# A two-layer transformer block on one core: the end in another order, and twelve gated products moved from VectorE to GpSimd

## The chip, the cores and the metric

The kernel runs on one core of one Trainium2 chip. The metric is the device time of one execution in microseconds (us), as a median over the runs. Times inside the kernel come from one profiled execution; its clock starts with its first instruction.

## The reference

The input is x of shape (8, 256, 128): 8 sequences of 256 tokens, 128 features, float32. Four sub-layers follow one another, each with a residual and a layer norm without weights. Cut to what matters:

```python
x = _layernorm(x + _L0_attn_ref(x, ...))   # 16 heads of 8, full softmax
x = _layernorm(x + _L0_ffn_ref(x, ...))    # expand to 512, butterflies, gelu
x = _layernorm(x + _L1_attn_ref(x, ...))   # low-rank q, k, v, rope, causal softmax
x = _layernorm(x + _L1_ffn_ref(x, ...))

def _L1_ffn_ref(x, w_gate, w_up, w_down):  # integer weights times 1/127
    gate = jnp.einsum('bsd,hd->bsh', x, wg)    # 128 -> 384
    up = jnp.einsum('bsd,hd->bsh', x, wu)
    h = jax.nn.silu(gate) * up
    return jnp.einsum('bsh,dh->bsd', h, wd)    # 384 -> 128
```

The change concerns the last of these, the gated feed-forward layer of layer 1, and the order of the last steps.

## The kernel before, in words

The program is written out by hand for five engines: TensorE, ScalarE (`act`), VectorE (`dve`), GpSimd (`pool`) and SyncE (`sp`, transfers). Each engine has its own instruction order; semaphores hold them together. A semaphore is counted up by an instruction with `then_inc`, and `wait_ge` holds an engine until a count is reached. Everything that stands behind a wait in that engine's order waits too.

The work is cut into 16 batches: batches 0 to 7 are the 8 sequences in layer 0, batches 8 to 15 the same sequences in layer 1. A batch has 16 heads, so there are 256 heads. All engines run the same loop `for g in STEPS` (`g` = 0, 4, 8, ... 288), one step for four heads (QUAD). In a step with `g` below 256 TensorE computes the scores of heads g to g+3, and, 12 heads ahead (LEAD), those from which VectorE takes the maxima (L864 in layer 0, L872 in layer 1, where a masked copy is needed); ScalarE takes the exponentials (L760). In layer 1 GpSimd sets what the causal mask hides to zero (L1083), one step later. Every other piece of work hangs on the step `g` = 16 b + offset of batch b, on all engines: value products (L632) with VectorE's transposes (L954), normalisation of the attention on GpSimd (L1090) with a transpose on VectorE (L969), projection out (L608), residual and statistics (L946, L833), layer norm on GpSimd (`normalise`, L1017 to L1024), turning of the tokens on TensorE (L561) with the copy on ScalarE (L773). The order of the `if` blocks inside a step is the order within that step on each engine. The rotation of queries and keys (L1137 to L1139), the subtraction of their high parts (L1063) and VectorE's small high/low subtraction of the maxima (L887) prepare later batches; there are no batches after 15, so they stop with g = 212 on GpSimd.

The feed-forward layer of layer 1 is set by the table FFN1 (L52 to L54): for each batch three offsets for its three chunks of 128 hidden features, one for the down matmuls, and one for the layer norm. For batch b and chunk c, with i = 3 (b - 8) + c:

- TensorE (L578 to L588) claims a bank and does four matmuls in 128x256 pieces, gate features into columns 0 to 255 and up features into 256 to 511. The bank's next user waits for `hid_ready`.
- ScalarE (L785 to L791) takes tanh of half the gate into `th` (two buffers).
- VectorE (`gate`, L889 to L901) makes `gated` = (th + 1) * gate, waits for itself (`link`), and multiplies it by the up features in the bank into `hid1`. The factor 0.5 of silu lies in the down weights. `th`, `gated` and `hid1` have two buffers each (`hid1` by batch).
- TensorE (L589 to L599) does the down matmuls from `hid1`; VectorE adds the residual (L935) and takes statistics; GpSimd normalises at the third number of the table; SyncE stores the batch.

Four gates of batches 13 and 14 are issued by VectorE at steps of their own (`LATE_GATES`, L56, L995), at the end of steps 260, 264 and 268. Up to step 252 a bank for such work is given by place; from step 256 on all banks are claimed in turn, eight of them. At the end of the kernel: step 264 on TensorE has the ups of (14,1), the down matmuls of batch 13 and the projection out of batch 15, in this order; step 268 the turn of batch 15 and the ups of (14,2); step 272 the ups of batch 15; steps 276 and 280 the down matmuls of batches 14 and 15. The layer norm of the attention of batch 15 and the last two of the feed-forward layer are divided: GpSimd takes the power -0.5, VectorE the subtraction and multiplication (`normalise_last`, L843).

In the profile `gated` appears as `room_c` (it shares that room with other tiles), `hid1` as `hid`, and all PSUM banks as `bank`.

Of the kernel before, what the change touches and what calls it, by code (L numbers as in the profile page):

```python
# [52 lines left out]
FFN1.update({BATCHES - 4: ((40, 40, 52), 60, 64), BATCHES - 3: ((40, 44, 52), 56, 64),  # L53
             BATCHES - 2: ((36, 40, 44), 52, 56), BATCHES - 1: ((32, 32, 32), 40, 44)})  # L54
# [70 lines left out]
def ffn1_at(g, i):  # L125

    for b in FFN1:
        if g == H * b + FFN1[b][i]:
            return b
    return None  # L130

# [19 lines left out]
def block_kernel(nc, x_nat, x_t, wfirst, bfirst, wqk0, wv0, bqk0, bv0, wproj, bproj, u0, d0, fac_u, fac_d, bfw, bup, bcon, bdown,  # L151
# [7 lines left out]
    with ctx:  # L159
# [3 lines left out]
        def sem(name):  # L163
            return ctx.enter_context(nc.semaphore(name))
# [19 lines left out]
        def part(room, first, shape):  # L184
# [83 lines left out]
            "up_ps", "th_ready", "hid_ready", "down_ps", "res_done", "var_ready", "ln_ready")}  # L268
# [3 lines left out]
        stored = [sem(f"stored{i}") for i in range(2)]  # L272

# [8 lines left out]
        def layer(b):  # L282
            return b // NB
# [69 lines left out]
        def _(pe):  # L353
# [172 lines left out]


# [18 lines left out]
            for g in STEPS:  # L546
# [10 lines left out]
                if (b := turned_at(g)) is not None:  # L557
                    bank = claim(("xt", b), A["xt_ready"], b + 1, g)
                    pe.wait_ge(A["ln_ready"], b + 1)
                    for q in range(QT):  # L560
                        ins = nc.tensor.transpose(bank[:, q * P:(q + 1) * P], NA["ln"][:, b % LN_RING, q, :], id32[:, :])  # L561
                    ins.then_inc(A["xt_ps"], 1)
# [15 lines left out]
                for b, c in ups_at(g):  # L578
                    i = b - NB
                    bank = claim(("up1", i, c), F1["hid_ready"], SC * i + c + 1, g)  # L580
                    if c == 0:
                        pe.wait_ge(A["xt_ready"], b + 1)
                        if i == 0:
                            pe.wait_ge(wf_ready, 2)
                    for s in range(2):
                        ins = nc.tensor.matmul(bank[:, s * T:(s + 1) * T], wf[:, s, c * P:(c + 1) * P],  # L586
                                               xt[:, i * T:(i + 1) * T], start=True, stop=True)
                    ins.then_inc(F1["up_ps"], 1)  # L588
                if (b := ffn1_at(g, 1)) is not None:  # L589
                    i = b - NB  # L590
                    bank = claim(("dn1", i), F1["res_done"], i + 1, g)
                    pe.wait_ge(F1["hid_ready"], SC * (i + 1) - (1 if b == BATCHES - 1 else 0))
                    for q in range(QT):
                        for c in range(SC):
                            if q == 0 and c == SC - 1 and b == BATCHES - 1:
                                pe.wait_ge(F1["hid_ready"], SC * (i + 1))
                            ins = nc.tensor.matmul(bank[:, q * W:(q + 1) * W], hid1[:, i % 2, c, q * P:(q + 1) * P],  # L597
                                                   wf[:, 2, c * W:(c + 1) * W], start=(c == 0), stop=(c == SC - 1))
                    ins.then_inc(F1["down_ps"], 1)  # L599
                if (b := attention_at(g, AT_PROJ)) is not None:  # L600
                    bank = claim(("proj", b), A["res_done"], b + 1, g)
                    pe.wait_ge(A["att_ready"], b + 1)
                    if b == 0:
                        pe.wait_ge(ld["bv"], 32)
                    elif b == NB:
                        pe.wait_ge(ld["next"], 64)
                    for q in range(QT):
                        ins = nc.tensor.matmul(bank[:, q * P:(q + 1) * P], att[:, q * P:(q + 1) * P],  # L608
                                               (wproj_sb if layer(b) == 0 else wout_sb)[:, :], start=True, stop=True)
                    ins.then_inc(A["proj_ps"], 1)  # L610
# [73 lines left out]
        def _(act):  # L684
# [68 lines left out]
            for g in STEPS:  # L753
# [31 lines left out]
                for b, c in ups_at(g):  # L785
                    i = SC * (b - NB) + c
                    act.wait_ge(F1["up_ps"], i + 1)
                    if i >= 2:
                        act.wait_ge(F1["hid_ready"], i - 1)
                    act.activation(th[:, i % 2, :], g_bank["up1", b - NB, c][:, 0:T], ACT.Tanh, scale=0.5)\  # L790
                        .then_inc(F1["th_ready"], 1)  # L791
# [30 lines left out]
        def _(dve):  # L822
# [66 lines left out]
            def gate(b, c):  # L889
# [3 lines left out]
                dve.wait_ge(F1["th_ready"], i + 1)  # L893
                if c == 0 and b >= NB + 2:
                    dve.wait_ge(F1["down_ps"], b - NB - 1)
                if i >= 2:
                    dve.wait_ge(F1["hid_ready"], i - 1)
                link(nc.vector.scalar_tensor_tensor(out=gated[:, i % 2, :], in0=th[:, i % 2, :], scalar=1.0,  # L898
                                                    in1=bank[:, 0:T], op0=ALU.add, op1=ALU.mult))
# [107 lines left out]
        def _(pool):  # L1007
# [62 lines left out]
            for g in STEPS:  # L1070
# [26 lines left out]
                if (b := ffn1_at(g, 2)) is not None and b >= HURRY:  # L1097
                    pool.wait_ge(F1["var_ready"], b - NB + 1)
                    inverse(N1 if b < BATCHES - 1 else NL, QT).then_inc(last_ready, 1)
                if (b := attention_at(g, AT_LN)) is not None and b < BATCHES - 1:  # L1100
# [193 lines left out]
```

## Time and profile before

| what | value |
|---|---|
| median of 3 runs | 326.21 us (324.72 to 326.78) |
| the profiled execution's own time | 325.87 us |
| its span, first to last instruction | 324.1 us |
| mean granted TensorE clock | 0.959 |
| TensorE busy | 275.0 us (85%) |
| VectorE busy | 253.7 us (78%) |
| ScalarE busy | 216.5 us (67%) |
| GpSimd busy | 205.3 us (63%) |

Busy is the time in which an engine has an instruction under way; shares are of the span and are means over stages that differ. The granted clock is 1.00 at 2.4 GHz and 0.50 at 1.2 GHz. "A <- B" in a list of waits means that engine and line A stood still until B was done. Matmuls are pipelined, so their ends are modelled.

### The profile page before, as it was taken

The page shows a single profiled execution, that of the slowest core. Times are in us where ns is not written, and L with a number is a line of the kernel's source. Part 1 is how long each engine was busy: PE and PEld are TensorE (multiplying, and loading weights), DVE is VectorE, ACT ScalarE, POOL GpSimd, SP SyncE. Part 2 cuts the span into 40 slices and gives each one's busy share as a digit, 9 for nine tenths or more (in the row PEclk, how much of TensorE's full clock was granted, in tenths as well). Part 3 has the DMA queues.
Part 4 walks back from the last instruction along what each step waited for, and adds up shares of the span by engine and source line. Part 5 has one row for each costly group of instructions (what it writes and reads, how often), then busy time and mean ns, then how long its engine had stood idle before and what let it go on. Part 6 is the DMA issues. An engine that isn't in the chain of part 4 may idle for free.

```text
span 324.1 us, 9463 instructions
## 1 busy us (share of the span) xinstructions
PE 275.0 (85%) x3194; PEld 200.0 (62%) x3194; DVE 253.7 (78%) x991; ACT 216.5 (67%) x444; POOL 205.3 (63%) x326
## 2 busy tenths in 40 slices
PE   8989969988978999888998896988898787878763
PEld 4766646655565556554676565866676666667553
DVE  4778796886878778897676697598999999775555
ACT  2546883788976799499983999468685757444110
POOL 0529995472448546584779897498879747366332
PEclk9979997999999999999995999899999999899978
DMA  7784350303021130404013140401314040000000
GB/s 228 258 254 144 93 192 15 131 1 131 3 97 35 32 133 17 150 4 155 8 46 120 23 145 11 153 1 41 126 35 148 3 148 20 2 2 18 17 16 32
DMA packets 20495, 25.84 MB, mean 80 GB/s; under 512 B 3744, under 2 KB 14304, under 8 KB 20320
## 3 DMA queue, kind: packets, MB, share of 16 engines
q1 hardware_dynamic: 20016, 24.72, 22.9%
q8 instruction: 26, 0.43, 0.6%
q10 hardware_dynamic: 432, 0.53, 0.4%
q14 instruction: 21, 0.17, 0.2%
HBM read 6.36 MB, written 1.05 MB: 23 GB/s over the span
## 4 chain that ended last, share of the span: by engine, by line
PE 51%; DVE 25%; issue 12%; ACT 9%; POOL 2%; POOLq 0%; ACTq 0%; DVEq 0%
PE bank L632 14%; DVE mx L864 6%; PE bank L388 5%; PE bank L647 4%; DVE room_c L872 4%; ACT E L760 4%; PE bank L398 4%; PE bank L576 4%; PE bank L515 2%; PE bank L597 2%; DVE room_c L898 2%; PE bank L407 2%; PE bank L586 2%; DVE turned L954 2%; PE bank L608 2%
## 5 line engine op out<-in xcount | busy, mean ns | idle before, releaser
L760 ACT ACTIVATE E<-bank 128x512 f32<-128x512 f32 (+1 forms) x256 | 119.7, 549 | 65.4 <-PE bank L411 37.9
L864 DVE TENSOR_REDUCE mx<-bank 128x2 f32<-128x512 f32 x128 | 79.6, 681 | 13.0 <-PE bank L388 12.8
L872 DVE CUSTOM_DVE_ANT_0 room_c<-bank,mask_sb 128x256 f32<-128x256 f32 (+1 forms) x256 | 72.9, 349 | 2.3 <-PE bank L388 2.1
L388 PE MATMUL bank<-QK 32*128 32x256 f32 x480 | 56.0, 308 | 8.4 <-DVE mx L872 3.4
L398 PE MATMUL bank<-QK 32*128 32x256 f32 x480 | 51.8, 311 | 11.5 <-DVE hid L900 6.7
L632 PE MATMUL bank<-E,V 128*32 128x256 f32 (+1 forms) x1024 | 59.5, 376 | 0.2
L388 PEld LDWEIGHTS bank<-QK 32*128 32x128 f32 x480 | 38.4, 187 | 21.4 <-issue 8.9
L1083 POOL TENSOR_SCALAR_AFFINE_SELECT E<-E 128x512 f32<-128x512 f32 x64 | 39.2, 638 | 11.6 <-ACT E L760 11.6
L398 PEld LDWEIGHTS bank<-QK 32*128 32x128 f32 x480 | 35.1, 188 | 17.5 <-DVE hid L900 9.0
L632 PEld LDWEIGHTS bank<-E,V 128*32 128x32 f32 x1024 | 31.0, 115 | 20.7 <-issue 3.6
L954 DVE STREAM_TRANSPOSE turned<-bank 128x256 f32<-128x256 f32 x32 | 14.3, 447 | 21.2 <-PE bank L632 20.9
L407 PE MATMUL bank<-mt,const_r 32*128 32x512 f32 x128 | 26.9, 435 | 4.0 <-ACT mt L704 4.0
L1063 POOL TENSOR_TENSOR parts<-qk,parts 128x512 f32<-128x512 f32 x15 | 19.2, 1278 | 14.9 <-ACT parts L730 14.9
L586 PE MATMUL bank<-xt,wf 128*128 128x256 f32 x96 | 25.6, 410 | 2.1 <-ACT E L760 1.6
L1090 POOL TENSOR_TENSOR at<-turned,rec 128x256 f32<-128x256 f32 x16 | 10.1, 632 | 26.2 <-DVE rec L976 26.2
L411 PE MATMUL bank<-mt,const_r 32*128 32x256 f32 (+1 forms) x256 | 22.9, 281 | 0.0
L586 PEld LDWEIGHTS bank<-xt,wf 128*128 128x128 f32 x96 | 18.4, 202 | 5.8 <-ACT E L760 2.8
L872 DVE DVE_READ_ACCUMULATOR2_ANT mx<- 128x1 f32 x256 | 21.2, 83 | 0.0
L1021 POOL TENSOR_SCALAR nm_a<-mv_a 128x2 f32<-128x2 f32 x15 | 2.9, 194 | 28.3 <-DVE mv_a L836 28.3
L411 PEld LDWEIGHTS bank<-mt,const_r 32*128 32x128 f32 x256 | 18.7, 195 | 0.2 <-ACT mt L704 0.2
L767 ACT ACTIVATE QK<-spread_qk 128x1024 fp32r<-128x1024 f32 x16 | 17.2, 1078 | 0.0
L647 PE MATMUL bank<-down,room_a 128*128 128x128 f32 x128 | 17.0, 288 | 0.0
(127 smaller groups left out, 561.7 us busy)
## 6 DMA issues: line engine op xcount, KB each, us to landing
spread_qk<-parts SPq DMA_DIRECT2D x30, 256.0 KB, 2.5
spread_qk<-parts SPq DMA_DIRECT2D x60, 128.0 KB, 2.2
room_c<-room_c SPq DMA_DIRECT2D x64, 32.0 KB, 1.9
xb<-x_nat SPq DMA_DIRECT2D x1, 1024.0 KB, 7.1
out<-ln_g SPq DMA_DIRECT2D x7, 128.0 KB, 1.9
xt<-x_t SPq DMA_DIRECT2D x1, 768.0 KB, 7.1
wi<-wi_all SPq DMA_DIRECT2D x1, 576.0 KB, 3.5
room_c<-fac_u SPq DMA_DIRECT2D x1, 508.0 KB, 6.4
```

The lines of the kernel that those rows point to most:

```text
L388: ins = nc.tensor.matmul(g_bank["max", m][:, cols], both[:, 0, c * P:(c + 1) * P], both[:, 1, keys], start=True, stop=True)
L398: nc.tensor.matmul(g_bank["exp", m][:, c * T:(c + 1) * T - q0], both[:, 1, c * P:(c + 1) * P], both[:, 0, q0:T], start=(c == 0), stop=False)
L407: ins = nc.tensor.matmul(g_bank["exp", m][:, :].rearrange("p (c t) -> p c t", c=2), ones, most.unsqueeze(1).broadcast_to([STRIP, 2, T]), s ...
L411: ins = nc.tensor.matmul(g_bank["exp", m][:, c * T:(c + 1) * T - c * P], ones, most[:, c * P:T], start=False, stop=(c == 1))
L586: ins = nc.tensor.matmul(bank[:, s * T:(s + 1) * T], wf[:, s, c * P:(c + 1) * P], xt[:, i * T:(i + 1) * T], start=True, stop=True)
L632: ins = nc.tensor.matmul(bank[VCOL * j:VCOL * (j + 1), q0:T], values, E[:, (2 * n + e) % E_RING, j, k * T:(k + 1) * T - q0], start=(e == 0 ...
L647: ins = nc.tensor.matmul(bank[:, i * W:(i + 1) * W], hid0[:, c, s * P:(s + 1) * P], down[:, c, :], start=(c == 0), stop=(c == HC - 1))
L760: act.activation(E[:, a % E_RING, j, 0:n], g_bank["exp", m][:, 0:n], ACT.Exp, scale=SCALE)\
L864: ins = nc.vector.tensor_reduce(mx[:, n % 2, :, i], bank[:, :].rearrange("p (q k) -> p q k", q=QT), AX.X, ALU.max, negate=True)
L872: ins = nc.vector.tensor_tensor_reduce(out=masked_s[:, at % 2, lo:hi], in0=bank[:, lo:hi], in1=mask_sb[:, T + lo - hi:T], scale=-1.0, scal ...
L954: nc.vector.transpose(turned[:, t, :], g_bank["pv", n][:, 0:T]).then_inc(A["turned"], 1)
L1083: nc.gpsimd.affine_select(out=e, in_=e, pattern=[[0, 4], [1, P]], compare_op=ALU.is_ge, fill=0.0, base=0, channel_multiplier=-1).then_inc( ...
```

## The change

Three things are changed. The table FFN1 puts the down matmuls of batch 13 at step 268 instead of 264, and the ups of (14,2) at step 264 instead of 268. In TensorE's order of a step the projection out of batch 15 now comes ahead of turns, ups and downs, and the turn of batch 15 behind the down matmuls. So step 264 has the projection of batch 15, ups (14,1), ups (14,2); step 268 the down matmuls of batch 13 and then the turn of batch 15. VectorE's residual and statistics of batch 13 move to step 268 with them, behind the last normalisation of the attention.

For batches 8 to 11 (SHARED; 12 chunks) ScalarE first copies the up features from the bank into `hid1` and then takes the tanh; VectorE does only the first of the gate's two instructions and frees the bank; GpSimd multiplies `hid1` in place by `gated`, one step later, ahead of its layer norm of the attention and of the rotation. Batches 12 to 15 keep both instructions on VectorE.

```diff
-             BATCHES - 4: ((40, 40, 52), 60, 64), BATCHES - 3: ((40, 44, 52), 56, 64),
-             BATCHES - 2: ((36, 40, 44), 52, 56), BATCHES - 1: ((32, 32, 32), 40, 44)})
+             BATCHES - 4: ((40, 40, 52), 60, 64), BATCHES - 3: ((40, 44, 52), 60, 64),
+             BATCHES - 2: ((36, 40, 40), 52, 56), BATCHES - 1: ((32, 32, 32), 40, 44)})
+
+SHARED = range(NB, BATCHES - 4)
...
+def shared(i):
+
+    return i // SC + NB in SHARED
...
+        def hidden_done(i):
+
+            return (F1["product"], i + 1) if shared(i) else (F1["hid_ready"], i + 1 - SC * len(SHARED))
+
+        def gate_done(i):
+
+            return (F1["gated"], i + 1) if shared(i) else hidden_done(i)
...
-                if (b := turned_at(g)) is not None:
...
+                if (b := turned_at(g)) is not None and b < BATCHES - 1:
+                    turn_tokens(b, g)
+
+                if attention_at(g, AT_PROJ) == BATCHES - 1:
+                    project_out(BATCHES - 1, g)
...
-                    bank = claim(("up1", i, c), F1["hid_ready"], SC * i + c + 1, g)
+                    bank = claim(("up1", i, c), *gate_done(SC * i + c), g)
...
-                    pe.wait_ge(F1["hid_ready"], SC * (i + 1) - (1 if b == BATCHES - 1 else 0))
+                    pe.wait_ge(*hidden_done(SC * i + SC - (2 if b == BATCHES - 1 else 1)))
...
-                if (b := attention_at(g, AT_PROJ)) is not None:
...
+                if turned_at(g) == BATCHES - 1:
+                    turn_tokens(BATCHES - 1, g)
+                if (b := attention_at(g, AT_PROJ)) is not None and b < BATCHES - 1:
+                    project_out(b, g)
...
                     act.wait_ge(F1["up_ps"], i + 1)
+                    if shared(i):
+                        if c == 0 and b >= NB + 2:
+                            act.wait_ge(F1["down_ps"], b - NB - 1)
+                        act.activation(hid1[:, b % 2, c, :], g_bank["up1", b - NB, c][:, T:2 * T], ACT.Copy)
                     if i >= 2:
-                        act.wait_ge(F1["hid_ready"], i - 1)
+                        act.wait_ge(*gate_done(i - 2))
...
                 dve.wait_ge(F1["th_ready"], i + 1)
+                if i >= 2:
+                    dve.wait_ge(*hidden_done(i - 2))
+                ins = nc.vector.scalar_tensor_tensor(out=gated[:, i % 2, :], in0=th[:, i % 2, :], scalar=1.0,
+                                                     in1=bank[:, 0:T], op0=ALU.add, op1=ALU.mult)
+                if shared(i):
+                    ins.then_inc(F1["gated"], 1)
+                    return
+                link(ins)
...
+                for b, c in ups_at(g - QUAD):
+                    i = SC * (b - NB) + c
+                    if shared(i):
+                        pool.wait_ge(F1["gated"], i + 1)
+                        nc.gpsimd.tensor_tensor(hid1[:, b % 2, c, :], hid1[:, b % 2, c, :], gated[:, i % 2, :], ALU.mult)\
+                            .then_inc(F1["product"], 1)
```

## Rows read from the trace of the kernel before

**Rows 1.** Windows, two periods of layer 1; columns as the header says.
```profile
core 0: us, PE busy (x) PEld busy (x) DVE busy (x) ACT busy (x) POOL busy (x), PEclk, DMA share, GB/s
...
246.00:262.60 16.60, 13.69 (x198) 11.08 (x198) 15.96 (x89) 11.51 (x26) 13.10 (x23) 1.00 0.19 68
262.60:279.30 16.70, 13.73 (x198) 11.17 (x199) 16.07 (x89) 10.98 (x25) 9.34 (x19) 1.00 0.11 35
```
**Rows 2.** Waits, 207.6 to 259.7 us: us in total, times, longest us.
```profile
POOL at L1090 <- DVE rec L976: 5.1, 2, 4.3
PE bank L398 <- DVE hid L900: 4.6, 4, 1.4
POOL nm_g L1021 <- DVE mv_g L836: 2.9, 2, 1.5
...
POOL nm_a L1021 <- DVE mv_a L836: 1.3, 2, 0.9
```
**Rows 3.** Timeline of VectorE: start us, us, line, operation, out<-in, count.
```profile
260.85 0.41 DVE L898 SCALAR_TENSOR_TENSOR room_c<-th,bank 128x256 f32<-128x256 f32 x1
261.29 0.42 DVE L900 TENSOR_TENSOR hid<-bank,room_c 128x256 f32<-128x256 f32 x1
261.63 0.41 DVE L898 SCALAR_TENSOR_TENSOR room_c<-th,bank 128x256 f32<-128x256 f32 x1
...
262.42 0.43 DVE L969 STREAM_TRANSPOSE att<-at 128x256 f32<-128x256 f32 x1
```
**Rows 4.** Timeline of ScalarE, the same pair of gates.
```profile
259.76 0.38 ACT L790 ACTIVATE th<-bank 128x256 f32<-128x256 f32 x1
260.63 0.38 ACT L790 ACTIVATE th<-bank 128x256 f32<-128x256 f32 x1 [0.48 <-PE bank L586]
```
**Rows 5.** Source lines L1090, L1114, L1063 of GpSimd: duration ns min/median/max, starts, forms.
```profile
L1090 POOL TENSOR_TENSOR at<-turned,rec x16: 629/632/637, 39.6 to 302.9; 128x256 f32<-128x256 f32 x16
...
L1114 POOL TENSOR_TENSOR xb<-ln_a,bcon_sb x8: 724/736/747, 57.7 to 181.9; 128x256 f32<-128x256 f32 x8
...
L1063 POOL TENSOR_TENSOR parts<-qk,parts x15: 1267/1278/1301, 9.9 to 257.2; 128x512 f32<-128x512 f32 x15
```
**Rows 6.** Timelines of GpSimd and TensorE around two hand-overs.
```profile
219.11 0.88 POOL L1024 TENSOR_SCALAR ln_a<-r_a,nm_a,rstd_a 128x128 f32<-128x128 f32 x2
...
221.49 0.44 PE L561 MATMUL bank<-const_sb,ln_a 128*128 128x128 f32 x2
...
259.67 0.64 POOL L1090 TENSOR_TENSOR at<-turned,rec 128x256 f32<-128x256 f32 x1
```
**Rows 7.** Source line L887 of VectorE, the small high/low subtraction.
```profile
L887 DVE TENSOR_TENSOR mxp<-mx,mxp x32: 175/382/1205, 16.2 to 287.1; 128x16 fp32r<-128x16 f32 x32
```
**Rows 8.** Timeline of TensorE at the end.
```profile
304.92 1.58 PE L597 MATMUL bank<-wf,hid 128*128 128x128 f32 x12 [0.93 <-DVE hid L900]
306.33 0.61 PE L608 MATMUL bank<-wout_sb,att 128*128 128x128 f32 x4
310.58 0.41 PE L561 MATMUL bank<-const_sb,ln_a 128*128 128x128 f32 x2 [3.64 <-DVE ln_a L843]
310.82 5.30 PE L586 MATMUL bank<-xt,wf 128*128 128x256 f32 x16
```
**Rows 9.** Timeline of VectorE at the end.
```profile
303.56 0.45 DVE L969 STREAM_TRANSPOSE att<-at 128x256 f32<-128x256 f32 x1 [1.63 <-POOL at L1090]
...
306.98 0.42 DVE L946 TENSOR_TENSOR r_a<-bank,xb 128x256 f32<-128x256 f32 x1
307.32 0.48 DVE L833 BATCH_NORM_STATS2 stats_g<-r_g 128x6 f32<-128x128 f32 x2
...
309.83 0.60 DVE L843 TENSOR_SCALAR ln_a<-r_a,mv_a,rstd_a 128x128 f32<-128x128 f32 x2 [0.33 <-POOL rstd_a L1018]
...
318.85 0.42 DVE L935 TENSOR_TENSOR r_l<-bank,ln_a 128x256 f32<-128x256 f32 x1
```
**Rows 10.** Windows, two stretches at a granted clock of 0.50.
```profile
280.70:284.10 3.40, 3.40 (x45) 2.05 (x48) 1.88 (x11) 0.51 (x2) 1.22 (x2) 0.50 0.02 5
...
311.40:314.80 3.40, 3.40 (x10) 2.69 (x9) 1.28 (x4) 0.78 (x3) 0.60 (x2) 0.50 0.12 39
```

More of the change, by code:

```diff
@@ L52 @@
 FFN1 = {b: ((40, 40, 48), 64, 68) for b in range(NB, BATCHES)}
[L53 to L54 removed]
+FFN1.update({BATCHES - 4: ((40, 40, 52), 60, 64), BATCHES - 3: ((40, 44, 52), 60, 64),
+             BATCHES - 2: ((36, 40, 40), 52, 56), BATCHES - 1: ((32, 32, 32), 40, 44)})
+SHARED = range(NB, BATCHES - 4)
 LATE_GATES = {(BATCHES - 3, 2): HEADS + 4, (BATCHES - 2, 0): HEADS + 8, (BATCHES - 2, 1): HEADS + 12, (BATCHES - 2, 2): HEADS + 12}
@@ L267, in block_kernel @@
         F1 = {n: sem(f"f1_{n}") for n in (
-            "up_ps", "th_ready", "hid_ready", "down_ps", "res_done", "var_ready", "ln_ready")}
+            "up_ps", "th_ready", "gated", "product", "hid_ready", "down_ps", "res_done", "var_ready", "ln_ready")}
         spread_in = sem("spread_in")
@@ L525, in project_values, with turn_tokens, project_out @@
                 ins.then_inc(A["v_ps"], 1)
+            def turn_tokens(b, g):
+                bank = claim(("xt", b), A["xt_ready"], b + 1, g)
+                pe.wait_ge(A["ln_ready"], b + 1)
+                for q in range(QT):
+                    ins = nc.tensor.transpose(bank[:, q * P:(q + 1) * P], NA["ln"][:, b % LN_RING, q, :], id32[:, :])
+                ins.then_inc(A["xt_ps"], 1)
+            def project_out(b, g):
+                bank = claim(("proj", b), A["res_done"], b + 1, g)
+                pe.wait_ge(A["att_ready"], b + 1)
+                if b == 0:
+                    pe.wait_ge(ld["bv"], 32)
+                elif b == NB:
+                    pe.wait_ge(ld["next"], 64)
+                for q in range(QT):
+                    ins = nc.tensor.matmul(bank[:, q * P:(q + 1) * P], att[:, q * P:(q + 1) * P],
+                                           (wproj_sb if layer(b) == 0 else wout_sb)[:, :], start=True, stop=True)
+                ins.then_inc(A["proj_ps"], 1)
             pe.wait_ge(idle_ready, 1)
@@ L556, in _ @@
                     project(b, claim(("qk", b), semaphore, value, g))
-                if (b := turned_at(g)) is not None:
[L558 to L562, printed above, removed]
+                if (b := turned_at(g)) is not None and b < BATCHES - 1:
+                    turn_tokens(b, g)
+                if attention_at(g, AT_PROJ) == BATCHES - 1:
+                    project_out(BATCHES - 1, g)
                 if (n := tile_at(g, AT_XT0)) is not None:
@@ L595, in _ @@
                             if q == 0 and c == SC - 1 and b == BATCHES - 1:
-                                pe.wait_ge(F1["hid_ready"], SC * (i + 1))
+                                pe.wait_ge(*hidden_done(SC * i + SC - 1))
                             ins = nc.tensor.matmul(bank[:, q * W:(q + 1) * W], hid1[:, i % 2, c, q * P:(q + 1) * P],
@@ L599, in _ @@
                     ins.then_inc(F1["down_ps"], 1)
-                if (b := attention_at(g, AT_PROJ)) is not None:
[L601 to L610, printed above, removed]
+                if turned_at(g) == BATCHES - 1:
+                    turn_tokens(BATCHES - 1, g)
+                if (b := attention_at(g, AT_PROJ)) is not None and b < BATCHES - 1:
+                    project_out(b, g)
                 if (b := values_at(g)) is not None:
@@ L893, in gate @@
                 dve.wait_ge(F1["th_ready"], i + 1)
+                if i >= 2:
[6 more added lines that the diff above has]
+                link(ins)
                 if c == 0 and b >= NB + 2:
                     dve.wait_ge(F1["down_ps"], b - NB - 1)
[L896 to L899, printed above, removed]
                 nc.vector.tensor_tensor(hid1[:, b % 2, c, :], bank[:, T:2 * T], gated[:, i % 2, :], ALU.mult)\
```

## The prediction

> **What bounds the kernel now.** I read the windows by stage first, then who waited for whom, then the timelines of the engines, and for the end the chain that ended last. The profiled execution has a span of 324.1 us and a time of 325.87 us, 0.34 us under the median of the three runs (326.21 us), so I work in the span and add the difference to the median.
>
> Both edits touch only what comes after about 207 us. From there to 280 us, one batch of layer 1 takes one period of 16.6 to 16.7 us, and in a period VectorE is busy 96% of the time, TensorE 13.7 us, ScalarE 11.0 to 11.5 us [rows 1]. The waits say the same: TensorE waits for the product of the gate before a bank comes free, 4.6 us in four waits between 207.6 and 259.7 us [rows 2]. GpSimd is the engine to watch: 13.1 us busy in the period from 246 us, but 9.3 us in the next, which has no rotation of queries and keys any more [rows 1]. From 207.54 us, where it stopped waiting (the longer of the two waits for rec), until 259.67 us its whole idle time is 5.1 - 4.3 + 2.9 + 1.3 = 5.0 us [rows 2]. At the end, from 301 us, no engine is full: one batch goes through proj, norm, turn, up, gate, down in a line, and what stands in front of it in an engine's order counts.
>
> **Shared products: VectorE.** A gate of before is a scalar_tensor_tensor and, after a wait for its own engine, a tensor_tensor. In the pair of gates (11,0), (11,1) the instructions start at 260.85 and 261.29, the second gate at 261.63, and the next one at 262.42 [rows 3]: the first of a gate takes 0.44, the second 0.34 us, and the second gate 0.79 in all. The change leaves one instruction, whose pitch without the chained wait is 0.34 us: 0.44 us less per gate, 12 gates, 5.3 us.
>
> **ScalarE.** The copy of the up half has the shape of a tanh row, 128x256 from PSUM, 0.38 us [rows 4]; bounds 0.26 (if it overlaps its neighbour by a third) and 0.41. The first copy of a pair has cover: its tanh starts at 259.76 and VectorE gets to it at 260.85. The second has less: the matmuls let it start at 260.63, so its tanh ends at 261.0 now and 261.3 to 261.4 after, against 261.19 when VectorE would want it. I charge 0.1 us a pair, with 0.2 at most. What is left of the pair is 0.77 us, and 0.43 us of the third gate, 1.2 us a batch, 4.8 us for four. TensorE's wait in front of the next scores, 1.0 to 1.4 us, is longer than that, so it does not become the bound there. The bank is released after the gate instruction instead of after the product, which is the same instant by which VectorE is earlier.
>
> **GpSimd.** Twelve products of 128x256 with both operands in SBUF. The nearest rows are the attention's multiplication, 0.632 us, and the addition of a bias, 0.736; the 512-column subtraction takes 1.278, which is the upper end for one product [rows 5]. I take 0.64 us, with a pitch of 0.59 since consecutive GpSimd rows overlap by about 0.05. The lower end is VectorE's own 0.42 us [rows 3]. Nine products fall in front of the attention normalisation of batch 12 (259.67 us [rows 6]): 9 x 0.59 = 5.3 us, against 5.0 us of idle time. So GpSimd has no idle time left there, and this normalisation ends not at 260.31 but at 260.31 + 0.3 = 260.6 us. Behind it stand VectorE's transpose of the result (262.42 now) and everything after: it can come at 260.6, 1.8 us earlier, not 0.77 x 4 + 0.43 x 3 = 4.4 us earlier. So two fifths of that gain arrive. On the way there is one more collision: in batch 9, ln_a ends at 219.99 (start 219.11, 0.88 us) and TensorE turns it at 221.49 [rows 6]. With two products ahead of it ln_a ends near 221.2, while TensorE, 1.1 us earlier, wants it at 220.4; 0.8 us of gain are given back there, but they are not on the path if GpSimd is the bound. Behind batch 12's normalisation GpSimd is free again (9.3 us busy [rows 1]), and the third gate of batch 11 adds its 0.43. Shared part: 1.8 + 0.4 = 2.2 us.
>
> The multiplication on GpSimd takes 0.632 us where VectorE took 0.42 [rows 3, 5]: half as much again. The Trainium skill (GPSIMD Engine Reference, Engine selection) gives elementwise products to VectorE and calls GpSimd about 2x slower with two inputs; by that ratio a product would be an estimated 0.85 us and the shared part 9 x 0.21 = 1.9 us poorer, near nothing. I hold to the row. The Trainium skill (GPSIMD Engine Reference, Key points) has the two engines contend for SBUF where VectorE has two SBUF inputs. The small high/low subtraction is such an instruction, and its rows vary from 175 to 1205 ns with a median of 382 [rows 7], which fits. The gates read PSUM and are steady at 0.41 and 0.42 us.
>
> The waits that are added: ScalarE's copy of a first chunk waits for the down matmuls of two batches before, over 10 us past. A product waits for its gate, which is one GpSimd step old; behind it in GpSimd's order stand the layer norm of the attention, the rotation of queries and keys (which ScalarE's next copy of the projection and SyncE's transfers wait for), and the masks, without which the value matmuls can't start. A TensorE bank waits for the gate alone, the down matmuls for the product, 12 heads or more after it is issued.
>
> **The end in another order.** Before, TensorE does up (14,1) and down 13 (304.92, 1.58 us, held until the gate of (13,2)) before the projection of batch 15, at 306.33 [rows 8]. Its input, VectorE's transpose, is done at 303.56 + 0.45 = 304.01 [rows 9]. After, it goes first: 304.15 to 304.75, and the residual of batch 15 starts at 304.8 instead of 306.98, now without down 13's residual (0.42 us) and statistics in front. From residual to ln_a it is 2.85 us now, of which down 13's statistics (307.32, 0.48 us and their aggregation [rows 9]) take some 0.6, so 2.25 after: ln_a would start at 307.05 instead of 309.83, 2.8 us earlier. TensorE meanwhile has up (14,1) and (14,2), 8 matmuls or 2.0 us, and down 13, 1.5 us: 304.75 + 3.5 = 308.25. So the new order makes down 13 the last to hold back the turn, at 308.3 instead of 310.58: 2.3 us earlier. Then up (14,2), four of the 16 matmuls at 310.82, is out of the way: 12 remain, 3.1 us at the full clock, from 309.2 (copy of the turned tokens) to 312.3. Of the 5.30 us of the 16, 3.4 us ran at a granted clock of 0.50, the 1.2 GHz level (311.40 to 314.80 [rows 10]), behind a TensorE wait of 3.64 us that the new order fills. GpSimd's layer norm of batch 13 keeps its step, ends some 2 us after VectorE's statistics at 309.5, and only the residual of down 14 needs it, at 313.7. VectorE then has down 13's residual and statistics (308.3 to 309.5) and five gates of 0.8 us: 313.5, as late as TensorE's ups allow. Down 14 and 15 go 312.3 to 315.1, so the last residual starts at 315.2 instead of 318.85 [rows 9]: 3.7 us earlier at the full clock; with half clock for 3.4 us somewhere in it, 2.7. I take 3.4.
>
> **Sum.** 2.2 + 3.4 = 5.6 us: 325.87 - 5.6 = 320.3 in the profiled execution, 326.2 - 5.6 = 320.6 us as median.
>
> **Rivals.**
> (A) The sharing gives nothing, the end does. For it: GpSimd's 5.0 us of idle time lie in five pieces, each behind a wait of its own, and a product of 0.736 us instead (pitch 0.69) costs 0.9 us more; add the 0.8 us of ln_a. Against: the pieces are in order with the products. 326.2 - 3.4 = 322.8 us.
> (B) GpSimd is not the bound (products at VectorE's 0.42: 9 x 0.42 = 3.8 us, under 5.0). Then VectorE's gain of 4.8 us arrives less the 0.4 of collisions: 326.2 - 4.4 - 3.4 = 318.4 us.
> (C) The end gives half: turn and ups wait for down 13, or another stretch of half clock as the one at 280.70, in which TensorE was busy all 3.4 us [rows 10]. 326.2 - 2.2 - 1.7 = 322.3 us.
> (D) GpSimd becomes the bound and costs more than the rest brings. Place: attention normalisation of batches 10 to 12. At 1.24 us pitch the nine products take 11.2 us, 5.9 more than above, and a TensorE that waits so long falls to half clock as behind 3.64 us here [rows 8, 10], at most half of 3.4 us. 320.6 + 5.9 + 1.7 = 328.2 us. It decides from 1.2 us a product. Against: two rows of this size at 0.63 and 0.74.
>
> **How the numbers follow.** Forecast 0.47, A 0.19, B 0.13, C 0.16, D 0.05. A measurement of this kernel tells about 1% (3.3 us): faster below 322.9. The forecast, B, two thirds of C and half of A are faster (0.47 + 0.13 + 0.10 + 0.09 = 0.79); slower half of D, 0.03; the rest, 0.18, is the same. The range reaches from B's 318.4 less 0.6 to A with 0.8 us more: 317.8 to 323.6.
>
> **What would show it.** The scalar_tensor_tensor x24 with tensor_tensor only x12; twelve GpSimd products of 0.60 to 0.75 us; GpSimd without idle time from 207.5 to the multiplication of batch 12, near 260; the period of TensorE's wait at the pair of gates under 16.3 us and that wait near 0.5 us; a turn of batch 9 that waits for ln_a; in the last 25 us proj of batch 15 before down 13, no TensorE wait of 3 us behind it, and last residual to end of span unchanged at 5.3 us. It is wrong if the periods stay at 16.7 us (A), if products take over 0.8 us (D), or if the turn of batch 15 comes less than 1.5 us earlier against the attention's last transpose (C).

## The result and the profile after

The changed kernel takes 318.59 us (median of 6 runs, 317.29 to 319.34); the kernel before, run beside it, takes 325.47 us. The ratio is 0.977, 95% interval 0.974 to 0.980: 2.3% faster. The forecast was 320.6 us, with a range of 317.8 to 323.6. Some executions of any of these kernels run some per cent longer at a lower clock: the ratios leave them out, the medians hold them.

The page of the changed kernel, its span and its busy times:

```profile
span 317.1 us, 9471 instructions
...
PE 273.0 (86%) x3194; PEld 198.9 (63%) x3194; DVE 249.8 (79%) x979; ACT 219.5 (69%) x456; POOL 213.7 (67%) x338
...
PE 44%; DVE 19%; POOL 14%; issue 11%; ACT 9%; POOLq 0%; ACTq 0%; DVEq 0%
```

The last line is the chain that ended last, by engine. GpSimd has 14% of the span in it; before it had 2%. VectorE has 12 instructions fewer, ScalarE and GpSimd have 12 more.

Where the 7.0 us of span went is read best from five instructions that both kernels have: the attention's multiplication on GpSimd for batch 9, and VectorE's transposes (att) behind that multiplication for batches 12, 13, 14 and 15. Their start times, taken from the timelines, cut the span into six parts (us):

| kernel | start to mult. 9 | to att 12 | granted clock there | to att 13 | to att 14 | to att 15 | to the end |
|---|---|---|---|---|---|---|---|
| before | 207.54 | 54.88 | 1.00 | 16.65 | 13.31 | 11.18 | 20.54 |
| after | 207.20 | 54.55 | 0.97 | 16.19 | 11.81 | 11.17 | 16.18 |
| difference | -0.34 | -0.33 | | -0.46 | -1.50 | -0.01 | -4.36 |

The first part is the same work in both and its 0.34 us are no part of the change. The 1.50 us in front of att 14 are the half-clock stretch of [rows 10] at 280.70, which this execution has elsewhere. So the profiled pair shows 0.8 us for the sharing, 4.4 us for the end (the half-clock stretch behind the turn of batch 15 is in it, since it too is gone), and 1.5 us of clock elsewhere.

The windows of the changed kernel, the whole shared stretch, a half-clock stretch in it, two periods, and the end:

```profile
core 0: us, PE busy (x) PEld busy (x) DVE busy (x) ACT busy (x) POOL busy (x), PEclk, DMA share, GB/s
222.30:225.70 3.40, 3.25 (x53) 2.26 (x42) 1.62 (x9) 0.86 (x3) 3.40 (x5) 0.50 0.22 48
245.30:261.90 16.60, 13.51 (x198) 10.99 (x196) 15.36 (x85) 12.59 (x31) 16.00 (x27) 1.00 0.19 67
261.90:278.40 16.50, 13.95 (x204) 11.41 (x207) 15.94 (x89) 11.27 (x27) 12.41 (x24) 1.00 0.19 65
...
300.90:311.80 10.90, 9.66 (x62) 8.62 (x62) 9.73 (x32) 2.31 (x7) 2.86 (x7) 1.00 0.07 25
```

Against [rows 1], GpSimd is busy for 16.0 of the 16.6 us in the period from 245 us, where it was 13.1, and VectorE went from 16.0 to 15.4. Who waited for whom between 207.3 and 261.1 us (us in total, times, longest):

```profile
POOL at L1125 <- DVE rec L1011: 4.3, 1, 4.3
...
PE bank L413 <- DVE room_c L927: 2.3, 4, 0.8
PE bank L547 <- POOL ln_a L1059: 1.9, 2, 1.0
...
POOL hid L1139 <- DVE room_c L927: 0.7, 1, 0.7
```

The waits behind mv_g and mv_a of [rows 2] are gone: GpSimd is late for them now. The wait for rec is the one of 4.3 us in front of the stretch, so GpSimd's time in waits fell from 5.0 to 0.7 us. TensorE waits for the bank 2.3 us instead of 4.6, and a new wait stands there, 1.9 us for ln_a before the turn of the tokens.

The product's own row, the source line on GpSimd:

```profile
L1139 POOL TENSOR_TENSOR hid<-hid,room_c x12: 728/734/745, 212.4 to 269.5; 128x256 f32<-128x256 f32 x12
```

It takes 0.734 us, not 0.64 as forecast. The timelines around the pair of gates (11,0), (11,1), VectorE and then GpSimd, answer to [rows 3] and [rows 6]:

```profile
261.07 0.74 DVE L927 SCALAR_TENSOR_TENSOR room_c<-th,bank 128x256 f32<-128x256 f32 x2
261.75 0.45 DVE L1004 STREAM_TRANSPOSE att<-at 128x256 f32<-128x256 f32 x1
```
```profile
229.01 1.42 POOL L1139 TENSOR_TENSOR hid<-hid,room_c 128x256 f32<-128x256 f32 x2 [0.65 <-DVE room_c L927]
...
261.09 0.63 POOL L1125 TENSOR_TENSOR at<-turned,rec 128x256 f32<-128x256 f32 x1
```

Two gates and the step to the transpose take 0.68 us on VectorE instead of 1.57. The attention's multiplication of batch 12, at 259.67 before, is at 261.09: 1.76 us later counted from that of batch 9 (53.89 instead of 52.13 us), and the transpose follows it by 0.66 us instead of 2.75.

ScalarE at the first shared pair, to compare with [rows 4]:

```profile
208.75 0.38 ACT L818 ACTIVATE hid<-bank 128x256 f32<-128x256 f32 x1
209.03 0.38 ACT L821 ACTIVATE th<-bank 128x256 f32<-128x256 f32 x1
209.61 0.38 ACT L818 ACTIVATE hid<-bank 128x256 f32<-128x256 f32 x1 [0.20 <-PE bank L620]
209.89 0.38 ACT L821 ACTIVATE th<-bank 128x256 f32<-128x256 f32 x1
```

A copy delays its tanh by 0.28 us. The end, TensorE and VectorE, answers to [rows 8] and [rows 9]:

```profile
301.51 0.68 PE L558 MATMUL bank<-wout_sb,att 128*128 128x128 f32 x4 [1.02 <-DVE att L1004]
302.03 1.89 PE L620 MATMUL bank<-xt,wf 128*128 128x256 f32 x8
303.76 1.50 PE L631 MATMUL bank<-wf,hid 128*128 128x128 f32 x12
305.31 0.41 PE L547 MATMUL bank<-const_sb,ln_a 128*128 128x128 f32 x2
306.29 2.83 PE L620 MATMUL bank<-xt,wf 128*128 128x256 f32 x12 [0.56 <-ACT xt L800]
```
```profile
300.92 0.45 DVE L1004 STREAM_TRANSPOSE att<-at 128x256 f32<-128x256 f32 x1 [1.62 <-POOL at L1125]
...
304.57 0.60 DVE L874 TENSOR_SCALAR ln_a<-r_a,mv_a,rstd_a 128x128 f32<-128x128 f32 x2 [0.34 <-POOL rstd_a L1053]
...
311.83 0.42 DVE L970 TENSOR_TENSOR r_l<-bank,ln_a 128x256 f32<-128x256 f32 x1
```

Counted from the transpose of batch 15, the projection starts after 0.59 us instead of 2.77, the turn after 4.39 instead of 7.02, and the last residual after 10.91 instead of 15.29. The wait of 3.64 us before the turn is gone, and the 12 ups behind it run at full clock.

### The profile page after: what moved, and what is told of

The parts are those of the page before. It is cut to its first block, busy times and chain, and to the rows that moved or that the text cites. A ratio compares the mean times of both kernels' runs of the same rounds, so it can differ in the third digit from the quotient of the medians.

```text
span 317.1 us, 9471 instructions
## 1 busy us (share of the span) xinstructions
PE 273.0 (86%) x3194; PEld 198.9 (63%) x3194; DVE 249.8 (79%) x979; ACT 219.5 (69%) x456; POOL 213.7 (67%) x338
## 4 chain that ended last, share of the span: by engine, by line
PE 44%; DVE 19%; POOL 14%; issue 11%; ACT 9%; POOLq 0%; ACTq 0%; DVEq 0%
PE bank L659 12%; DVE mx L895 5%; PE bank L403 5%; ACT E L787 4%; PE bank L610 4%; PE bank L674 4%; PE bank L413 3%; POOL E L1118 3%; DVE room_c L903 3%; PE bank L530 2%; PE bank L422 2%; DVE turned L989 2%; PE bank L620 2%; PE bank L631 2%; POOL hid L1139 2%
## 5 line engine op out<-in xcount | busy, mean ns | idle before, releaser
L620 PE MATMUL bank<-xt,wf 128*128 128x256 f32 x96 | 24.2, 390 | 2.4 <-ACT E L787 1.3
L620 PEld LDWEIGHTS bank<-xt,wf 128*128 128x128 f32 x96 | 17.2, 190 | 5.7 <-ACT E L787 2.5
```

## The experiments

In the tables "end" means the new order of the end (TensorE's order and the table), "sharing" the products on GpSimd. Where a set of batches is given, SHARED holds these and the semaphore counts follow from it. A ratio is against the kernel before on the same chip. The six parts of each span are collected in a table behind the last run. The runs were taken on three chips, and the kernel before had medians of 325.43, 324.67 and 326.36 us there, so between groups of runs the ratios are to be compared and not the medians.

**The two parts apart.** Sharing alone: table and TensorE's order as before.

```diff
-             BATCHES - 4: ((40, 40, 52), 60, 64), BATCHES - 3: ((40, 44, 52), 60, 64),
-             BATCHES - 2: ((36, 40, 40), 52, 56), BATCHES - 1: ((32, 32, 32), 40, 44)})
+             BATCHES - 4: ((40, 40, 52), 60, 64), BATCHES - 3: ((40, 44, 52), 56, 64),
+             BATCHES - 2: ((36, 40, 44), 52, 56), BATCHES - 1: ((32, 32, 32), 40, 44)})
...
-                if (b := turned_at(g)) is not None and b < BATCHES - 1:
+                if (b := turned_at(g)) is not None:
...
-                if (b := attention_at(g, AT_PROJ)) is not None and b < BATCHES - 1:
+                if (b := attention_at(g, AT_PROJ)) is not None:
```

> Only the shared products of batches 8 to 11; the end is that of before. Theory (GpSimd is the bound of batches 9 to 12, a product has a pitch of 0.70 us): VectorE's transpose in front of the projection of batch 12 comes only some 0.3 us earlier, the third gate of batch 11 adds 0.4, and what else there is comes from where the half-clock stretches fall: 0.8 to 2.5 us faster than before, near 324 us. Rival (VectorE's saved 4.8 us arrive): 321 us. Rival (sharing costs as much as it brings): 325.5 us, no change.

Measured: 322.40 us, ratio 0.990 (0.986 to 0.994), 3.0 us faster by the medians, 3.3 by the ratio: more than the theory allowed (0.8 to 2.5), less than the rival's 4.8. The end alone:

```diff
-SHARED = range(NB, BATCHES - 4)
+SHARED = ()
```

> Only the other order of the end; all 24 products on VectorE. Theory: the turn of batch 15 comes 2.6 us earlier against the attention's last transpose, the ups of batch 15 follow at full clock: 3.7 to 4.4 us faster than before, near 321.3 us, and no half-clock stretch behind the turn. Rival (the end gives half of that): 323.5 us. The sum of this gain and that of the sharing alone should be the 6.9 us of the whole change, within 0.7; more than that apart, the two parts help each other by the clock.

Measured: 321.80 us, ratio 0.989 (0.985 to 0.993), 3.7 us faster. The two ratios multiply to 0.979, the whole change has 0.977: the parts add up, each with about half. But the sharing brings 3 us here where the two traces showed 0.8. That gap is taken up behind the table of parts.

**The two halves of the end.** TensorE's order alone: the table of before, no sharing.

```diff
-             BATCHES - 4: ((40, 40, 52), 60, 64), BATCHES - 3: ((40, 44, 52), 60, 64),
-             BATCHES - 2: ((36, 40, 40), 52, 56), BATCHES - 1: ((32, 32, 32), 40, 44)})
+             BATCHES - 4: ((40, 40, 52), 60, 64), BATCHES - 3: ((40, 44, 52), 56, 64),
+             BATCHES - 2: ((36, 40, 44), 52, 56), BATCHES - 1: ((32, 32, 32), 40, 44)})
...
-SHARED = range(NB, BATCHES - 4)
+SHARED = ()
```

> TensorE's order of the end alone (projection of batch 15 first, its turn behind ups and downs); the table of before, no sharing. Theory: VectorE's order still has down 13's residual ahead of the projection's, and down 13 now comes after the projection, so the residual of batch 15 starts at about 307.7 instead of 307.0 and the turn is no earlier: within 1 us of before. Rival (TensorE's order is what counts): 2 us faster or more.

Measured: 326.62 us, ratio 1.002 (0.999 to 1.005): no change. Its VectorE timeline, with the transpose of batch 15 at 302.95:

```profile
306.47 0.42 DVE L975 TENSOR_TENSOR r_g<-bank,ln_a 128x256 f32<-128x256 f32 x1 [2.31 <-PE bank L636]
306.81 0.41 DVE L986 TENSOR_TENSOR r_a<-bank,xb 128x256 f32<-128x256 f32 x1
```

The projection is ready 0.6 us after the transpose, and VectorE waits 2.31 us for down 13 first, because its own order has that residual in front. The residual of batch 15 (r_a) comes 3.86 us after the transpose, 3.42 before the change. An engine's order was changed, and the order of the one behind it kept the gain. The clock has a share in the "no change" too: TensorE fell to half clock inside its wait of 3.10 us for ln_a, 0.6 us before the turn, and stayed there for 6.8 us, where the kernel before has 3.4 us:

```profile
309.80:316.60 6.80, 5.63 (x14) 4.32 (x15) 3.63 (x10) 1.43 (x4) 1.78 (x4) 0.50 0.06 19
```

Its 12 ups behind the turn took 5.29 us for it, and 2.83 us in the changed kernel. The table alone:

```diff
-                if (b := turned_at(g)) is not None and b < BATCHES - 1:
+                if (b := turned_at(g)) is not None:
...
-                if (b := attention_at(g, AT_PROJ)) is not None and b < BATCHES - 1:
+                if (b := attention_at(g, AT_PROJ)) is not None:
...
-SHARED = range(NB, BATCHES - 4)
+SHARED = ()
```

> The table alone (down 13 one step later, ups (14,2) one step earlier); TensorE's order within a step as before, no sharing. Theory: the projection of batch 15 waits for 8 up matmuls instead of 4 and down 13, and goes 0.7 to 1.3 us earlier than before; TensorE then stands idle until the turn, which is 2 us earlier, and down 13 comes behind it, in front of the ups of batch 15: 2 to 2.6 us faster than before, 1.2 us or more slower than both parts together. Rival (the table is nothing without the order): no change.

Measured: 323.44 us, ratio 0.996 (0.992 to 0.999), 1.4 us faster by the ratio: a gain, smaller than expected. Its TensorE timeline and one window at the end:

```profile
308.51 0.66 PE L552 MATMUL bank<-const_sb,ln_a 128*128 128x128 f32 x2 [3.12 <-DVE ln_a L874]
308.96 2.77 PE L633 MATMUL bank<-wf,hid 128*128 128x128 f32 x12
```
```profile
308.60:312.00 3.40, 3.40 (x16) 3.31 (x17) 0.23 (x1) 0.38 (x1) 0.00 (x0) 0.50 0.00 0
```

The turn comes 4.86 us after the transpose (7.02 before), as worked out. Then down 13 runs behind it at half clock, 2.77 us instead of 1.5, in front of the ups, and these run at half clock for the most part too, 4.10 us instead of 2.83. The low clock lasts for 6.8 us here, from 307.4 to 314.2 us, and makes these two groups 2.5 us longer; before, it made the 16 ups behind the turn 1.7 us longer (5.30 us against 3.62 us for the 16 ups at 301.33 us of this run). The difference, 0.8 us, is about what the gain falls short of the expectation. The table is what frees the projection's path on VectorE; TensorE's order is what puts down 13 into the wait for ln_a, and it needs the table to bring the turn forward.

**Where sharing pays.** All runs of this and the next group have the new end.

```diff
-SHARED = range(NB, BATCHES - 4)
+SHARED = (11, 12)
```

> The new end, but the shared products are those of batches 11 and 12 instead of 8 to 11: six products, none in front of the attention normalisation of batch 12. Theory (GpSimd has room only there): both batches bring their 1.2 us in full, 2.4 us below the kernel with the new end alone (321.8), near 319.4 us, so six products do as much as the twelve. Rival (the gain goes with VectorE's saved time, 0.44 us a gate): half of the twelve's gain, 1.6 us, 320.2 us.

Measured: 318.46 us, ratio 0.979 (0.976 to 0.983). Six products do what twelve do (318.59 us, 0.977), and somewhat more than the 2.4 us expected of them: 3.0 us by the ratios against the end alone. Its trace has the clock of before, 1.00, up to att 12, so the parts of the table can be compared directly: 0.84 us less to att 12, 1.29 to att 13, 0.19 to att 14 (against 11.80 us in the traces without a half-clock stretch there) and 0.46 more to att 15, 1.9 us in all. The other 1.1 us are in none of these parts, and where they come from stays open.

With `SHARED = (8, 9, 10)`:

> The new end and the shared products of batches 8, 9 and 10 only: nine products, all in front of batch 12's attention normalisation. Theory (GpSimd bound at a pitch of 0.70 us a product): the transpose behind that normalisation comes 0.3 to 0.7 us earlier and nothing is added later: 321.2 us, within 1 us of the new end alone, but for the clock's stretches. Rival (VectorE's time arrives): 3.6 us faster, 318.2 us.

Measured: 321.09 us, ratio 0.987 (0.982 to 0.991), against 0.989 with the end alone: nothing that can be told. The changed kernel's three further products, those of batch 11, are worth 1% against this run; the timelines show 1.4 us of it (the transpose follows the multiplication of batch 12 after 1.56 us here and 0.66 there, and the third gate brings its 0.46), the rest lies within the two intervals, and this run's part to att 13 holds a half-clock stretch (18.21 us). With `SHARED = (11, 12, 13)`:

> The new end and the shared products of batches 11, 12 and 13. Theory: as with 11 and 12; batch 13's gates stand where VectorE waits for tanh anyway (from 286 us on), so three more products bring nothing: within 0.7 us of the run with 11 and 12. Rival: another 1.2 us.

Measured: 319.84 us, ratio 0.982 (0.977 to 0.987). That is 1.4 us above the run with 11 and 12 on the same chip, where 0.7 was expected at most, but the two intervals overlap. The parts from att 12 on are those of the run with 11 and 12 within 0.1 us, so batch 13 brings nothing there; the part to att 12 is 2.1 us longer, at a mean clock of 0.94 instead of 1.00. The next two have three products in front of batch 12's multiplication, first `SHARED = (9, 11, 12)`:

> The new end and the shared products of batches 9, 11 and 12: three products (2.1 us) go into the 5.0 us that GpSimd stands idle in front of batch 12's attention normalisation, six behind it. Theory (GpSimd's idle time is the budget there): from the attention's multiplication of batch 9 to the transpose of batch 12 it takes 1.2 us less than with 11 and 12 alone, so 317.3 us, the fastest. Rival (the idle time lies behind waits and can't be used): 318.5 us or more, as with 11 and 12.

Measured: 317.12 us, ratio 0.972 (0.967 to 0.978). Then `SHARED = (10, 11, 12)`:

> The same with batch 10 in the place of 9. Theory: as with batch 9, 317.3 us, if the budget is one for the whole stretch. Rival: batch 10's products stand right ahead of batch 12's normalisation and of GpSimd's longest full stretch, so they cost more than batch 9's: 318.5 us.

Measured: 317.95 us, ratio 0.973 (0.968 to 0.977). Both have the lowest medians of the study, but their intervals overlap that of the changed kernel and of the run with 11 and 12. Whether batch 9 or 10 adds something is not settled: the stretch to att 12 takes 54.33 us with batch 9 at a mean clock of 0.97, and 54.04 without it at 1.00. The time with batch 9 came as expected, but the 1.2 us that the theory expected this stretch to be shorter are not seen in the traces, so the hit shows nothing of the mechanism. With batch 10 the stretch takes 56.03 us at 0.94.

**GpSimd's idle time.** Nine more multiplications, in front of the products of batches 8, 9 and 10, into a tile that is made for them:

```diff
                         pool.wait_ge(F1["gated"], i + 1)
+                        if i < 3 * SC:
+                            nc.gpsimd.tensor_tensor(spare[:, i, :], gated[:, i % 2, :], gated[:, i % 2, :], ALU.mult)
```

> The changed kernel with nine more GpSimd multiplications of the same size, one in front of each product of batches 8, 9 and 10, into a tile that nobody reads. Theory (GpSimd has no idle time left between the attention normalisations of batches 9 and 12): all nine pitches of 0.69 to 0.70 us show, 5.5 to 6.3 us, near 324.6 us. Rival (GpSimd still has slack; VectorE or TensorE is the bound): under 2 us, at most 320.6 us.

Measured: 323.82 us, ratio 0.996 (0.993 to 0.999), by the ratios 1.9% or 6 us above the changed kernel. The added instruction, and the window from the multiplication of batch 9 to that of batch 12:

```profile
L1141 POOL TENSOR_TENSOR spare<-room_c x9: 612/612/627, 209.0 to 257.5; 128x256 f32<-128x256 f32 x9
```
```profile
203.86:263.40 59.54, 50.37 (x604) 39.44 (x601) 48.15 (x271) 39.69 (x94) 56.47 (x90) 0.84 0.21 67
```

59.54 us against 53.89 is 5.65 us. The nine instructions have a pitch of 0.57 us, not the 0.69 to 0.70 expected, so they bring 5.1 us: every one of them shows. The rest is GpSimd's waits for its gates, which grew from 0.7 to 1.3 us. GpSimd is busy for 56.5 of the 59.5 us and is the bound of the stretch. The mean clock of TensorE is lower too, 0.84 against 0.97; what that costs here is at most the 0.6 us of longer waits.

**ScalarE's copy and the early release.** The twelve products back on VectorE, from the copy, and GpSimd's loop of products taken out:

```diff
                 if shared(i):
                     ins.then_inc(F1["gated"], 1)
+                    dve.wait_ge(F1["gated"], i + 1)
+                    nc.vector.tensor_tensor(hid1[:, b % 2, c, :], hid1[:, b % 2, c, :], gated[:, i % 2, :], ALU.mult)\
+                        .then_inc(F1["product"], 1)
                     return
```

> The changed kernel with the twelve products back on VectorE, but from ScalarE's copy in SBUF and with the bank given free before the product: ScalarE's twelve copies and the earlier release without GpSimd's part. Theory (the copies are hidden; VectorE's 0.44 us a gate and GpSimd's idle time are all that counts): within 1 us of the new end alone, 320.8 to 322.8 us. Rival (the copies delay tanh and cost): 323.5 us or more. Rival (the early release is what brings the gain): 319.5 us.

Measured: 323.41 us as median, ratio 0.989 (0.984 to 0.994), where the end alone has 0.989. The ratio speaks for the theory, the median is near the rival in which the copies cost: taken by the ratio, copy, early release and the new form of the product together are worth nothing that can be told. The product on VectorE, now with both inputs in SBUF:

```profile
L932 DVE TENSOR_TENSOR hid<-hid,room_c x12: 424/470/1124, 207.5 to 272.2; 128x256 f32<-128x256 f32 x12
```

With one input in the bank it was 424 to 426 ns in all 24 rows. The twelve together took 7.6 us here, 5.1 at 0.424 us each. So VectorE had some 2.5 us more to do, and a gain of up to that size from the early release could be hidden in this run; it does not rule the release out.

**The parts of all profiled executions** (us, as in the first table):

| run | to mult. 9 | to att 12 | clock there | to att 13 | to att 14 | to att 15 | to the end |
|---|---|---|---|---|---|---|---|
| sharing alone | 205.49 | 55.49 | 0.94 | 16.18 | 11.78 | 11.17 | 20.59 |
| end alone | 205.85 | 58.44 | 0.94 | 18.62 | 11.78 | 11.16 | 16.25 |
| order alone | 204.24 | 59.07 | 0.91 | 16.68 | 11.79 | 11.17 | 21.95 |
| table alone | 207.08 | 56.92 | 0.94 | 16.68 | 11.81 | 11.16 | 19.95 |
| 11, 12 | 206.99 | 54.04 | 1.00 | 15.36 | 11.61 | 11.63 | 16.27 |
| 8, 9, 10 | 206.35 | 55.41 | 0.97 | 18.21 | 11.80 | 11.19 | 16.24 |
| 11, 12, 13 | 207.48 | 56.11 | 0.94 | 15.35 | 11.62 | 11.55 | 16.19 |
| 9, 11, 12 | 205.66 | 54.33 | 0.97 | 15.34 | 11.61 | 11.62 | 16.24 |
| 10, 11, 12 | 205.75 | 56.03 | 0.94 | 15.33 | 11.62 | 11.64 | 16.23 |
| nine more | 203.86 | 62.80 | 0.84 | 16.19 | 11.78 | 11.16 | 16.21 |
| products on VectorE | 203.90 | 60.92 | 0.92 | 16.42 | 11.78 | 11.17 | 16.21 |

Two things are seen here that single times hide. The parts are the same to 0.1 us from kernel to kernel wherever the work and the clock are the same. And the half-clock stretches fall in other places in each execution: the profile of before had none between 207 and 262 us, the end alone had its stretches there:

```profile
205.85:264.30 58.45, 48.64 (x624) 38.13 (x620) 52.40 (x286) 39.16 (x90) 47.02 (x75) 0.94 0.25 82
```

The corresponding windows of the changed kernel and of the sharing alone:

```profile
207.20:261.75 54.55, 46.84 (x624) 37.67 (x620) 48.83 (x274) 41.71 (x101) 52.10 (x83) 0.97 0.22 73
```
```profile
205.49:260.98 55.49, 48.56 (x624) 38.42 (x620) 47.62 (x275) 40.99 (x99) 52.88 (x84) 0.94 0.23 75
```

At a mean clock of 0.94 this stretch takes 56.9 and 58.4 us with the products on VectorE and 55.5 us with those of batches 8 to 11 on GpSimd; at 1.00 it took 54.88 before, and 54.55 us is what the changed kernel has at 0.97. From the multiplication of batch 9 to that of batch 12 the three kernels with these nine products need 53.89, 53.94 and 53.85 us, at mean clocks of 0.97, 0.94 and 0.97. So where GpSimd is the bound, a TensorE at half clock costs little, and where VectorE and TensorE take turns, a stretch seems to cost 1 to 2 us. This fits the gap between 0.8 us in the pair of traces and 3 us in the runs, since the profiled execution of before has no such stretch there. It rests on one profiled execution of each kernel and was not tested by itself. Equal mean clocks do not make equal times either: up to the multiplication of batch 12 the table alone takes 52.95 and the end alone 55.11 us, both at 0.94.

The recorded executions allow one more estimate. Over the 23 of the kernel before that ran beside the sharing alone, 0.01 of mean clock goes with 2.05 us of time (a straight line through them). The sharing alone had a mean clock of 0.960 where they had 0.955, which is 0.9 us by that line. So about 1 of its 3 us goes with less half clock, and 1.9 us are left at the same clock, more than the 0.8 us of the pair. With six executions against 23 this is rough, and how the gain of the sharing divides stays open.

## Why the prediction was right, point by point

The time lay 2.0 us under the forecast and inside the range. The gain was 6.9 us where 5.6 were forecast; the other 0.7 us came from the kernel before, whose median fell from 326.21 to 325.47 us with three more runs. That the number came this close is in part luck: in the profiled pair the sharing gave 1.4 us less than its term, the end 1.0 us more, and 1.5 us came from a term that the sum did not have.

**What bounds the kernel: right.** VectorE up to 280 us, GpSimd next to it, and nothing full at the end. GpSimd's 5.0 us of idle time in front of batch 12 were the budget: 0.7 us of waits are left, nine more instructions show in full, and nine products in front of that point gave nothing that can be told while six, none of them in front of it, gave all.

**VectorE's part: right.** 0.44 us a gate; the pair took 0.89 us less, the third gate of batch 11 brought 0.46 us (0.43). **ScalarE's part: right**, though its tanh is later by 0.28 us and VectorE waited for one of them (0.49 us, batch 9). **The turn of batch 9 waits for ln_a: right**, 1.0 us (0.8).

**The price of a product: mis-sized.** The step was "the nearest rows are the attention's multiplication, 0.632 us". The right row of the two was the other, 0.736 us: the product takes 0.734, with a pitch of 0.70. Nine times 0.11 us is 1.0 us. The prediction had this price in its rival A, at 0.9 us. A second term was missing: the products of batch 9 waited 0.65 us for their gate, behind TensorE's half-clock stretch at 222 us. Together they put the multiplication of batch 12 1.76 us later than before, not 0.3. In the profiled pair the shared part gave 0.8 us instead of 2.2.

**The end: right in its mechanism, 1.0 us too small.** Projection 2.2 us earlier against the transpose (2.2 worked out), turn 2.6 (2.3), last residual 4.4 (3.7 at full clock, 3.4 taken). In the runs the end alone gave 3.7 us. The eight ups ran in 1.73 us instead of 2.0. The order-alone run shows why VectorE's order belongs to the sum: without it the same TensorE order brought the turn no earlier.

**The clock: the term that was missing.** It was priced only at the end. The stretch at 280 us was not there after the change, which gave 1.5 us in the pair. It is no effect of the change as far as is known: in all eleven other traces, some of them with the old end or without sharing, this part takes 11.6 to 11.8 us too. The stretches between 207 and 262 us seem to cost the changed kernel less. So the gain came out 1.3 us better than forecast by a shared part that was too large, an end that was too small and a clock that was not in the sum.

**The rivals.** A (the sharing gives nothing): 1.0% from the sharing alone is against it, though the profiled pair, with 0.8 us, comes near it. Its sign, periods that stay as they were, was there in the pair up to batch 12: VectorE's transposes of batches 9 and 12 are 50.8 us apart, 50.2 before, and only the period to batch 13 is shorter. B (GpSimd is not the bound): out. C (the end gives half): out. D (GpSimd costs more than the rest brings): its mechanism was shown with nine more instructions, which put the kernel back to 0.4% under the one before; at a pitch of 0.70 us a product it doesn't apply.

**The price by the ratio.** The Trainium skill (GPSIMD Engine Reference, Engine selection) speaks of about 2x for two inputs; the rows give 0.734 against 0.424 us, 1.7x, so the truth lay between the row that was taken and the rule. By the rule's estimate the shared part would have been 0.3 us; it was 0.8 in the pair of traces and 3 in the runs.

## What to carry to other kernels

Before moving work to an engine with free time, add up its idle time only up to the next point where the critical chain waits for it; here nine products in front of that point brought nothing that could be told, and six others, none of them in front of it, the whole gain. When an instruction is moved ahead in one engine's order, look at what stands ahead of its consumer in that engine's order too, or the gain stays there. Compare stretches of two traces only with their granted clock beside them: one execution's half-clock stretches are as large as the parts of such a change.

## What was not expected of the hardware

The four profiled executions in which TensorE waited over 3 us before the turn of batch 15 (before, sharing alone, order alone, table alone: 3.64, 3.64, 3.10 and 3.12 us) all fell to half clock near it, but not at the same place. Before and with the sharing alone the clock fell 0.8 and 1.3 us behind the start of the turn, with TensorE at work again, and was low for 3.4 us. With the order alone and with the table alone it fell inside the wait, 0.6 and 1.1 us before the turn, after some 2.5 and 2.0 us in which TensorE did nothing, and was low for 6.8 us.

All nine with the new end, whose longest wait there is 1.1 us, ran this part at a granted clock of 1.00. Elsewhere the stretches of 3.4 us changed their places from one execution to the next.

GpSimd's multiplication of 128x256 takes 0.612 us when both inputs are the same tile and the output another, and 0.734 us when they are two tiles in SBUF and one of them is the output. VectorE's product of the same size is steady at 424 to 426 ns with one input in the bank and goes from 424 to 1124 ns with both in SBUF, beside a busy GpSimd; that fits what the Trainium skill (GPSIMD Engine Reference, Key points) says of contention with two SBUF inputs, and the number beside it is a median of 470 ns. GpSimd seems to pay as well: its rotation instruction (room_c<-room_c,ropes_sb) at 226.49 us of that run, beside such a product, takes 1.46 us, where the eight of the kernel before take 1.28 to 1.31 us.
